# Chunks 9 to 15 of a state-space scan: decay matrix masked by GpSimd in place of the score matrix, S ahead of the state, partial sums dealt 3, 3 and 6

## What is computed

```
cs   = cumsum(dt * A)                                   # per head, within a chunk
tri  = tril(ones(Q, Q))
Ldec = where(tri, exp(cs[..., :, None] - cs[..., None, :]), 0)
att  = einsum('bchqn,bchkn->bchqk', Cc, Bc) * Ldec
Yd   = einsum('bchqk,bchkp->bchqp', att, Xc * dtc)      # within the chunk
states = einsum('bchq,bchqn,bchqp->bchpn', exp(cs[-1] - cs), Bc, Xc * dtc)
state(c+1) = exp(cs[-1]) * state(c) + states(c)
Yo   = einsum('bchqn,bchpn,bchq->bchqp', Cc, state, exp(cs))
y    = (Yd + Yo + D * x) * silu(z);   out = y @ w_out.T
```

## Time and profile before

| | us |
|---|---|
| median of 3 runs | 765.19 (765.18 to 767.17) |
| the profiled execution | 765.62 |
| its span | 763.9 |
| TensorE busy | 749.3 (98%) |
| VectorE busy | 630.1 (82%) |
| ScalarE busy | 449.8 (59%) |
| GpSimd busy | 338.5 (44%) |

### The profile page before, as it was taken

One profiled execution on the slowest core, in us unless ns is written; L12 is line 12 of the kernel. 1 busy time (PEld: TensorE's weight loads), 2 busy tenths in 40 slices (PEclk: granted clock), 3 DMA queues, 4 the chain that ended last, 5 costly groups with the idle time before them and its releaser, 6 DMA issues.

```text
span 763.9 us, 10500 instructions
## 1 busy us (share of the span) xinstructions
PE 749.3 (98%) x3370; PEld 349.6 (46%) x3370; DVE 630.1 (82%) x1241; ACT 449.8 (59%) x881; POOL 338.5 (44%) x392
## 2 busy tenths in 40 slices
PE   8999999999999999999999999999999999999998
PEld 3444544455544444444444444444444444444444
DVE  7798888878978979878799978878878878767994
ACT  4867877677786675643545556456456456444441
POOL 5631544664442379775414233243243233224574
PEclk9999999999999999999999999999999999999999
DMA  8943644563331133420521833733733743443475
GB/s 302 192 77 74 166 92 102 120 112 83 70 88 38 42 56 71 109 55 1 121 48 25 180 70 69 166 70 69 164 71 69 161 74 64 79 79 70 112 158 158
DMA packets 97413, 75.03 MB, mean 98 GB/s; under 512 B 65504, under 2 KB 72992, under 8 KB 97360
## 3 DMA queue, kind: packets, MB, share of 16 engines
q0 software_dynamic: 17280, 31.46, 23.0%
q1 hardware_dynamic: 77872, 39.70, 20.0%
q10 hardware_dynamic: 2208, 3.21, 1.6%
HBM read 23.46 MB, written 4.23 MB: 36 GB/s over the span
## 4 chain that ended last, share of the span: by engine, by line
PE 64%; DVE 19%; ACT 8%; issue 4%; DMA 2%; POOL 1%; ACTq 0%; DVEq 0%; SPq 0%; POOLq 0%
PE PS L2022 57%; DVE raw L1500 3%; PE PS L2145 2%; DVE stage L1500 2%; PE PS L2153 1%; DVE st L1332 1%; DMA x_t<-hb 1%; DVE state L1482 1%; DVE xs L1429 1%; ACT xds L871 1%; ACT pre L921 1%; ACT th L937 1%; ACT raw L922 1%; DVE S L1465 1%; DVE S L1871 1%
## 5 line engine op out<-in xcount | busy, mean ns | idle before, releaser
L733 POOL DMA_DIRECT2D xs<-x x59 | 51.1, 866 | 153.1 <-ACT x L1199 139.4
L2022 PE MATMUL PS<-h,w_in 128*128 128x512 f16 x480 | 108.7, 379 | 0.7 <-DMA h<-hn_p 0.7
L2022 PE MATMUL PS<-h,x_t 128*128 128x512 f16 x408 | 94.0, 379 | 0.0
L2022 PEld LDWEIGHTS PS<-h,w_in 128*128 128x128 f16 x480 | 46.9, 98 | 65.8 <-issue 15.8
L2022 PE MATMUL PS<-n_T,stage 128*128 128x512 f16 x288 | 71.5, 379 | 0.0
L1199 ACT ACTIVATE x<-PS,d_d 128x512 f32<-128x512 f32 x59 | 40.3, 683 | 38.9 <-PE PS L2022 38.9
L2022 PEld LDWEIGHTS PS<-h,x_t 128*128 128x128 f16 x408 | 39.5, 98 | 48.5 <-issue 2.5
L542 POOL TENSOR_TENSOR r<-mv,mhalf 128x1 f32<-128x1 f32 (+1 forms) x32 | 29.6, 926 | 65.4 <-DVE mv L1336 51.4
L733 POOL DMA_DIRECT2D xs<-n x29 | 25.3, 871 | 67.8 <-ACT n L1199 58.4
L2022 PE MATMUL PS<-pre,stage 128*128 128x512 f16 x192 | 49.3, 379 | 0.0
L1169 ACT ACTIVATE xds<-tm,dgh 128x512 f32<-128x512 f32 x24 | 17.4, 724 | 53.2 <-DVE tm L1946 53.2
(11 more groups left out here) (323 smaller groups left out, 1818.8 us busy)
## 6 DMA issues: line engine op xcount, KB each, us to landing
xs<-x POOLq DMA_DIRECT2D x75, 256.0 KB, 3.3
xs<-n POOLq DMA_DIRECT2D x29, 256.0 KB, 3.3
x_t<-x_in SPq DMA_DIRECT2D x16, 256.0 KB, 3.0
x_t<-hb POOLq DMA_DIRECT2D x16, 256.0 KB, 3.9
out<-x_t SPq DMA_DIRECT2D x15, 256.0 KB, 2.3
raw_gu<-gate_t SPq DMA_DIRECT2D x7, 512.0 KB, 4.4
raw_gu<-up_t SPq DMA_DIRECT2D x7, 512.0 KB, 6.3
raw_d<-down_t SPq DMA_DIRECT2D x7, 512.0 KB, 7.4
```

The costliest lines, as they stand in the source:

```text
L733: po.dma_start(chunk_of(xs, c), d_tmps[d % 3], accum_op=ALU.add).then_inc(s_acc[d % 3], 16)
L2022: ins = pe.matmul(out_, lhs(a, b, k), rhs(a, b, k), start=first and n == 0, stop=last and n == len(todo) - 1)
```

## The change

`FIRST_MASKED` is 9. For chunks 9 to 15 (made in steps 8 to 14):

- GpSimd masks `Ld` (new `scan_mask`, waits `e_Ld`, releases the new semaphore `e_Ldm`) ahead of `scan_c`; the mask of S in `scan_d` is dropped, the addition of D stays.
- ScalarE makes `Ld` right behind the late conv pieces, ahead of tanh pieces and of `hi2`.
- VectorE's `weights` waits for `e_Ldm`, and `weights` and `scan1` come ahead of `advance`, no longer behind it.
- `scan_c(12)` goes back from behind `rms2(10)` to its usual place, and the partial sums of GpSimd are 3, 3 and 6 in steps 10, 11 and 12 (before 3, 5 and 4). The fourth high and low part of the first group follows to a place behind the gate piece of step 12.

```diff
+        FIRST_MASKED = 2 * CH + 1
...
+            def scan_mask(c):
+                po.wait_ge(e_Ld, c + 1)
+                mask(Ld[:, :, :]).then_inc(e_Ldm, 1)
+
             def scan_d(c, j):
                 po.wait_ge(e_S, c + 1)
-                chain(po.affine_select(out=S[:, j % 2, :, :], in_=S[:, j % 2, :, :], compare_op=ALU.is_ge, fill=0.0,
-                                       base=0, pattern=[[0, H], [1, P]], channel_multiplier=-1))
+                if c < FIRST_MASKED:
+                    chain(mask(S[:, j % 2, :, :]))
                 po.tensor_tensor(S[:, j % 2, :, :], S[:, j % 2, :, :], d_diag[:, :, :], ALU.add).then_inc(e_SD, 1)
...
+                if c + 1 >= FIRST_MASKED and c + 1 < NCH:
+                    scan_mask(c + 1)
                 if c + 1 < NCH:
-                    if c != 2 * CH + 3:
-                        scan_c(c + 1, (c + 1) % CH)
+                    scan_c(c + 1, (c + 1) % CH)
...
-            T_EARLY = {2 * CH + 2: range(0, 3), 2 * CH + 3: range(3, 8), 3 * CH: range(8, 12),
+            T_EARLY = {2 * CH + 2: range(0, 3), 2 * CH + 3: range(3, 6), 3 * CH: range(6, 12),
...
+                if c + 1 >= FIRST_MASKED and c + 1 < NCH:
+                    scan_decay(c + 1, (c + 1) % CH)
+                if c > 0 and i_late < NS:
                     slot_b(i_late, late[0])
...
-                if c + 1 < NCH:
+                if c + 1 < FIRST_MASKED:
                     scan_decay(c + 1, (c + 1) % CH)
...
-                advance(c, j)
+                if c + 1 < FIRST_MASKED:
+                    advance(c, j)
                 if c + 1 < NCH:
                     weights(c + 1, (c + 1) % CH)
                     scan1(c + 1, (c + 1) % CH)
+                if c + 1 >= FIRST_MASKED:
+                    advance(c, j)
                 if c > 3 * CH:
                     lo2(c - 1)
                 if c == 3 * CH:
-                    t_los(0, 0, 1, 2, 3)
+                    t_los(0, 0, 1, 2)
...
+                if c == 3 * CH:
+                    t_los(0, 3)
```

More of the change, by code:

```diff
@@ L276, in build @@
             sem(n) for n in "e_sp_neg e_sp_exp e_dA e_cs_col e_xB_tr e_xB_T e_cs e_gap".split())
-        e_Ld, e_wv, e_ecs, e_G, e_S, e_SD, e_cs_cut, e_cs_b, e_cs_f, s_csd, s_cs = (
-            sem(n) for n in "e_Ld e_wv e_ecs e_G e_S e_SD e_cs_cut e_cs_b e_cs_f s_csd s_cs".split())
+        e_Ld, e_wv, e_ecs, e_G, e_S, e_SD, e_cs_cut, e_cs_b, e_cs_f, e_Ldm, s_csd, s_cs = (
+            sem(n) for n in "e_Ld e_wv e_ecs e_G e_S e_SD e_cs_cut e_cs_b e_cs_f e_Ldm s_csd s_cs".split())
         e_Cdec, e_xds, e_Y, e_y, e_dstate, e_state, e_n1, e_wo = (
@@ L568, in scan_c, with mask @@
                 po.tensor_tensor(xbc[s][:, 2:CB, cols], xbc[s][:, 2:CB, cols], ecs[:, j % 2, :, :], ALU.mult).then_inc(e_Cdec, 1)
+            def mask(t):
+                return po.affine_select(out=t, in_=t, compare_op=ALU.is_ge, fill=0.0,
+                                        base=0, pattern=[[0, H], [1, P]], channel_multiplier=-1)
+            def scan_mask(c):
+                po.wait_ge(e_Ld, c + 1)
+                mask(Ld[:, :, :]).then_inc(e_Ldm, 1)
             def scan_d(c, j):
                 po.wait_ge(e_S, c + 1)
-                chain(po.affine_select(out=S[:, j % 2, :, :], in_=S[:, j % 2, :, :], compare_op=ALU.is_ge, fill=0.0,
-                                       base=0, pattern=[[0, H], [1, P]], channel_multiplier=-1))
+                if c < FIRST_MASKED:
+                    chain(mask(S[:, j % 2, :, :]))
                 po.tensor_tensor(S[:, j % 2, :, :], S[:, j % 2, :, :], d_diag[:, :, :], ALU.add).then_inc(e_SD, 1)
@@ L657, in step @@
                 rms2(c, c % CH)
-                if c == 2 * CH + 2:
-                    scan_c(c + 2, (c + 2) % CH)
                 if not early_sums:
@@ L996, in step @@
                 if c == 3 * CH:
-                    t_his(0, 0, 1, 2, 3)
+                    t_his(0, 0, 1, 2)
                 renorm(c)
@@ L1009, in step @@
                     gate_b(0, j)
+                if c == 3 * CH:
+                    t_his(0, 3)
                 square(c, j)
@@ L1454, in weights @@
                 s = j % 2
-                ve.wait_ge(e_Ld, c + 1)
+                if c < FIRST_MASKED:
+                    ve.wait_ge(e_Ld, c + 1)
+                else:
+                    ve.wait_ge(e_Ldm, c + 1 - FIRST_MASKED)
                 ve.tensor_tensor(wv[:, s, :], Ld[:, :, P - 1:P].rearrange("p h o -> p (h o)"), dt[:, (c // CH) % 2, j * H:(j + 1) * H], ALU.mult).then_inc(e_wv, 1)
```

## The result

The changed kernel is slower: 769.57 us (769.25 to 770.02, 4 runs) against 765.18 (764.91 to 767.17, 4 runs) for the kernel before on the same chip. The ratio is 1.0058 with a 95% interval of 1.0046 to 1.0071, that is 4.4 us. The prediction said 764.9 and a range up to 767.2; it was wrong in sign and size. The profiled execution took 769.87 us.

What follows compares the result with a forecast made beforehand. TensorE's work plus its waits was taken as the bound, VectorE as the second. Of 5.15 us reachable waits, 4.9 would go and 4.6 new ones come: -0.3, so 764.9 us against the median of 765.19; range 762.0 to 767.2.

Steps and rivals of the forecast that it cites:

- Chunk 9 had no wait: nothing: Chunk 9, made in step 8: TensorE had no wait there, so no gain or loss was counted.
- between 0.4 us earlier and 0.4 later: Chunk 15: the fifth gate/up product starts that near 331.75, with S ending at 315.7 to 316.2.
- the sum's terms: Whole kernel: 4.9 us of TensorE's waits go and 4.6 us of new ones come, in sum -0.3.
- Chunk 10, gain of 0.6 to 1.2: Ahead of chunk 10's product: the shorter chain removes the 1.23 us wait, less contention; 1.0 us taken.
- The price set for taps beside GpSimd: Conv taps ahead of chunk 10: mask and `scan_c` beside them lengthen VectorE's taps, costing up to 0.6 us.
- Silu, chunk 12 and the bank of the first gate/up product: Waits of 0.55 and 0.75 us go; the first gate/up product then waits for `silu_z`, starting 1.3 to 1.9 us earlier.
- Step 12, on which the sum rested: Late `hi2(11)` and port meetings start the low parts 1.0 to 2.8 us later; chunk 13's output product at 304.2.
- The slower rival: Low parts after 292 aren't made good; fifth gate/up product 2.0 to 2.9 us late, 767.2 to 768.1; chance 0.16.
- a third place without slack: Two were named: chunk 13's output product behind `gate_y(13)`, and the fifth gate/up product behind its gated value.
- The last waits: Signs in the trace: no wait at chunks 10, 12, 13, 14; new ones for `silu_z` and, 1 to 4 us, `gate_y(13)`.
- the two signs of being wrong that it named: `w(13)` starting before 302, or TensorE still waiting for the addition at chunk 13 or 14.
- The rule on the port: VectorE instructions with two SBUF inputs and GpSimd ones reading SBUF exclude each other; meetings cost 0.64 to 1.38 us.

Runs made afterwards that it cites:

- With the mask back on S: The changed kernel with GpSimd's mask on S again, behind S, for chunks 9 to 15; 766.5 us, before 764.52.
- with `scan_c` ahead of the mask: The changed kernel with GpSimd's `scan_c` ahead of the mask of the same chunk in place of behind it; 769.39 us, ratio 1.0059.
- the kernel without chunk 9: The changed kernel with chunk 9 alone made as before; 767.97 us, ratio 1.0045.
- the kernel with only S ahead of the state: The kernel before with one part alone: `weights` and S ahead of the state for chunks 9 to 15; 766.81 us, ratio 1.002.
- the kernel with chunks 10 to 12: The kernel before with the whole new order for chunks 10, 11 and 12, sums 3, 5, 4; 765.9 us, ratio 1.0016.
- the matrix behind `hi2`: The changed kernel with ScalarE's decay matrix back behind the tanh pieces and `hi2`, the mask still on the matrix; 773.4 us, ratio 1.0109.
- the sums as before: The changed kernel with sums 3, 5, 4 and the fourth high and low part back in their place; 769.76 us, ratio 1.0058.
- chunks 10 and 11 alone: The kernel before with the whole new order for chunks 10 and 11 only, sums 3, 5, 4; 763.27 us, before 764.52, ratio 0.9986.

## Why the prediction was wrong, step by step

Two steps failed: "Chunk 9 had no wait: nothing", and the fifth gate/up product "between 0.4 us earlier and 0.4 later". In traces set to the same start that product is 4.7 us late, and 1.6 of it come from chunk 9, 0.2 by chunk 14 (a gain of 0.4 was forecast) and 2.9 in chunk 15. In the sum's terms: 5.15 us of waits were to shrink by 4.9 and 4.6 new ones to come. Of the old ones 2.1 us stayed (1.48, 0.17 and 0.43), and 6.4 came (0.82, 1.46, 1.68, 1.59 and 0.88), 3.4 us more waiting than before.

**Chunk 9, "nothing": wrong, 1.6 us.** The step asked only whether TensorE had waited there. But the edit also moves `hi2(7)` behind the matrix, and `lo2(7)` with it to beside the mask and `scan_c(9)`: the very two prices that were counted for step 12. Here is VectorE before, step 8:

```profile
225.50 0.98 DVE L1423 SCALAR_TENSOR_TENSOR h2n_p<-x,r,h2n_p 128x512 f16<-128x512 f32 x1 [1.45 <-ACT h2n_p L814]
```

It already waited 1.45 us for `hi2`; the changed kernel makes that 3.28, and `lo2` takes 1.85 instead of 0.98. The taps start 1.15 us later in trace time (232.04 for 230.89), 1.65 with the 0.5 by which this trace is ahead. Two runs divide this. With the mask back on S, and with `scan_c` ahead of the mask, the matrix is as early and `lo2` waits as long (3.27 us), but it takes 0.75 us, and the taps start 0.55 us later than before in either: at 230.13 with the silu of step 8 at 221.19, and at 230.97 with that silu at 222.04.

So `hi2` behind the matrix costs 0.55 us of the 1.65, and `lo2` beside `scan_c` the other 1.1.

**Chunk 10, gain of 0.6 to 1.2: right by itself, eaten by chunk 9.** In the kernel without chunk 9 the product is at 248.12; it was at 250.18, and this trace is 0.7 ahead (silu of step 8 at 221.83): 1.4 us won, all of the wait. The price set for taps beside GpSimd, up to 0.6, was paid on VectorE: the silu behind the taps starts at 243.00 before and at 242.85 in the kernel without chunk 9, which is 0.5 us later once 0.7 is added. TensorE didn't feel it, since the addition, begun at 246.78, still ended at 248.06, before the product at 248.12.

**Silu, chunk 12 and the bank of the first gate/up product: mechanism right, size at the edge.** Without chunk 9 the first gate/up product starts at 282.18, 1.2 us earlier than before after the same correction (1.3 to 1.9 predicted), and it waits 0.81 for `silu_z`, as foreseen. With chunk 9 it is 0.5 us later than before.

**Step 12, on which the sum rested: right.** Without chunk 9:

```profile
286.84 0.75 DVE L1444 SCALAR_TENSOR_TENSOR h2n_p<-x,r,h2n_p 128x512 f16<-128x512 f32 x1 [3.94 <-ACT h2n_p L830]
287.50 1.23 DVE L1480 TENSOR_TENSOR wv<-Ld,dt 128x4 f32<-128x4 f32 x1
...
290.72 0.95 DVE L1629 TENSOR_TENSOR w_in<-hn,w_in 128x512 f16<-128x512 f32 x1
...
302.61 0.74 DVE L1499 SCALAR_TENSOR_TENSOR raw<-PS,d_ih,raw 128x512 f32<-128x512 f32 x1
```

With the 0.7 us added by which this trace is ahead: `lo2` at 287.5 (predicted 286.9 to 287.5), low parts at 291.4 (290.4 to 292.2), `gate_y(13)` at 303.3 (taken at 303.5), the output product at 303.41 + 0.7 = 304.1 (304.2) and chunk 14's product at 307.75 + 0.7 = 308.4 (307.85; it waits 0.43 more for the addition). The contention on `wv` was in it. The changed kernel does the same 1.8 us later: low parts at 292.56, `gate_y(13)` at 304.44, output product at 305.23, chunk 14's product at 309.58. The slower rival's condition, low parts after 292, was so met, by a delay from step 8, which the rival hadn't named; its price of 2.0 to 2.9 us was too small, for the reason that follows. What the forecast missed even here is that the gate/up product of step 13 waits 1.46 us for the gated value (298.21), a third place without slack. It cost nothing by itself: with or without it the output product starts as `gate_y(13)` ends, 304.44 + 0.74 = 305.18. And chunk 14's S didn't come right behind `gate_y(13)`: `wv` waited 0.73 us for the mask and took 1.23, so the addition ended at 307.70 + 0.7 = 308.4 in place of 306.5. The mask was late for the reason that follows, too: ahead of it stood `rms2(12)`, 2.67 us from its first row to the mask (302.32 to 304.99 in the changed kernel).

**Chunk 15, "between 0.4 earlier and 0.4 later": wrong, 2.4 us.** Two terms. First, GpSimd was taken to be free for the mask at 313.74, but that is where `rms2(13)` starts; `ms`, `r` and the issue of a DMA follow. GpSimd in chunk 15 of the kernel without chunk 9:

```profile
313.75 0.19 POOL L592 TENSOR_SCALAR ms<-ssq 128x1 f32<-128x1 f32 x1
314.02 0.57 POOL L548 TENSOR_TENSOR r<-ms,mhalf 128x1 f32<-128x1 f32 x1
314.55 0.90 POOL L595 DMA_DIRECT2D xs<-x  x1
315.22 0.90 POOL L577 TENSOR_SCALAR_AFFINE_SELECT Ld<-Ld 128x512 f32<-128x512 f32 x1
```

and of the changed kernel, where sums and chunk 14 are later:

```profile
317.04 0.90 POOL L572 TENSOR_SCALAR_AFFINE_SELECT Ld<-Ld 128x512 f32<-128x512 f32 x1
317.65 1.52 POOL L569 TENSOR_TENSOR raw<-raw,ecs 128x512 f32<-128x512 f32 x1
```

From `ms` to the mask are 1.47 us: the row that was read was the first of three instructions ahead of the mask. Second, `wv` behind that mask meets `scan_c` and takes 1.23. So the mask starts at 315.2 or 317.0, and S ends at 318.4 or 320.2 in place of 315.7 to 316.2, in trace time, to which 0.7 or 0.5 us has to be added. ScalarE had the matrix at 315.84, so in the changed kernel 1.2 us of the wait of 3.08 is GpSimd's queue alone. Before, S was made as soon as ScalarE had the matrix, and GpSimd did `rms2(13)` and `scan_c` beside it.

**The last waits.** Predicted: no wait at chunks 10, 12, 13 and 14; measured 1.48, 0.17, none and 0.43. A new wait at the first gate/up product and one of 1 to 4 us at `w(13)`: both there, 0.82 and 1.68. The fifth gate/up product at 331.3 to 332.2: at 336.00. Of the two signs of being wrong that it named, one came: TensorE still waits for the addition at chunk 14.

**The rule on the port.** `wv`, two SBUF inputs, took 1.22 to 1.23 us in steps 11 to 14 and 0.15 to 0.16 in steps 8 to 10 of the changed kernel, where it met no `scan_c`; S, one input from PSUM, took 1.11 to 1.12 in each. With `scan_c` moved, `wv` fell to 0.16 and the `lo2` of step 8 from 1.85 to 0.75. That is as the Trainium skill has it ("SBUF — State Buffer", section "Who interferes with whom"): a VectorE instruction with two SBUF inputs and a GpSimd instruction that reads SBUF shut each other out, and the trace agrees in all these rows. So here two engines hold each other up where no semaphore stands between them. It was a price of the change, and the forecast held it for step 12 but not for steps 8 and 14.

**What stays open.** What chunks 13 and 14 cost singly, and what chunk 12 costs with the sums 3, 3 and 6: neither was tried. Nor was any run made that divides the 3.4 us up to `w(13)` between the early matrix, S ahead of the state and the meetings on the port.

## What to carry to other kernels

When an edit moves an instruction ahead of another on one engine, price the one that is now behind in every iteration that the edit reaches, and what it and its consumers now run beside, not only where the bottleneck waited: the 1.6 us of chunk 9 came from a step that had no wait to win, and two thirds of it from `lo2`, which stood where it had stood but now met another engine's work. When work moves to the front of an in-order queue, take the time at which the queue is free from the end of the last instruction ahead of it, its DMA issues too, and check whether the consumer of before overlapped that queue. An edit over a range is best tried on the part where the wait is: here two chunks of seven gave 1.3 us, and the other five took it back more than four times over.

## What the hardware showed that was not expected

The granted clock of TensorE fell behind a long wait, and the time didn't suffer. It was 1.00 in every stretch of 10 us of the kernels before and after; in the kernel with only S ahead of the state it wasn't (a stretch of 10 us: busy us of PE, PEld, DVE, ACT and POOL with counts, granted clock, DMA share, GB/s; the stretch before it has 1.00):

```profile
290.00:300.00 10.00, 7.33 (x21) 3.96 (x21) 9.96 (x16) 6.00 (x14) 9.68 (x8) 0.85 0.23 38
```

The TensorE rows in it:

```profile
296.30 1.44 PE L2147 MATMUL PS<-S,tm 128*128 128x512 f32 x2 [2.67 <-POOL S L588]
297.53 1.92 PE L2156 MATMUL PS<-raw,state 128*128 128x128 f32 x8
```

Elsewhere these take 1.12 and 1.05 us, and from the start of the product to the raw scores of the next chunk are 4.37 us here (296.30 to 300.67), 2.71 in the kernel before (294.33 to 297.04). The mean of 0.85 says that TensorE spent a part of the stretch at the lower of its two levels, 1.2 in place of 2.4 GHz, right behind an idle time of 2.67 us. The same came after 2.64 us in the kernel with chunks 10 to 12 (0.83 in its stretch from 290 us) and after 2.95 us with the matrix behind `hi2` (0.83 from 250 us), and not after 2.32 us with the sums as before (1.00 from 290 us). So TensorE lost another 1.7 us behind this wait; for the one of 2.64 us it is the same, for the one of 2.95 us 1.4 (254.05 to 258.30, before 250.18 to 253.00).

Yet the time doesn't show it. With only S ahead, VectorE's low parts begin at 291.49, 1.75 us later than before once the 0.4 is taken off, and that is ahead of the fall of the clock; the fifth gate/up product, at 333.78, is 1.7 us later. What TensorE lost in between went into its wait of 1.33 us ahead of chunk 14's product, which is gone in this trace. With chunks 10 to 12 it is the same: against chunks 10 and 11 alone the low parts are 2.8 us late and the fifth gate/up product 2.9. The record of every execution agrees. Each has its mean clock over the span, and it was 0.997 or 0.998 in some and 1.00 in others of the same kernel: with only S ahead 766.20 us (median of 7) against 766.84 (of 3), with chunks 10 to 12 766.03 (of 6) against 765.91 (of 4). So chunk 12's cost is that of the late engines, not of the clock. What decides whether the clock falls isn't shown: executions of one kernel differ in it. With the matrix behind `hi2` all four executions had 0.998, and what the clock cost there isn't shown.
